# The last output chain moves into the first experts, the weight split into the attention, and two norms share one power

## The reference, cut to what matters

```python
h = W.T[x] + b + positional                       # embedding
h = h + linear_attention(layernorm(h))            # 8 heads of 16, normalised scores, causal
z = layernorm(layernorm(h), gain, bias)           # two norms in a row
q, k, v = z @ Wq, z @ Wk, z @ Wv                  # 2 heads of 64
q, k = l2norm(q) * 8 * qn_g, l2norm(k) * 8 * kn_g
y = causal_softmax(q @ k.T / 8) @ v @ Wo
gate = softmax(y @ gate_W + gate_b)               # over 8 experts
h = h + sum_e gate_e * (gelu(y @ W1_e + b1_e) @ W2_e + b2_e)   # 128 -> 512 -> 128
```

## Time and profile before

| | us |
|---|---|
| median of three runs (lowest, highest) | 964.89 (957.13, 965.5) |
| profiled execution, its time | 964.4 |
| its span | 962.3 |
| PE busy | 827.2 (86%) |
| DVE busy | 732.0 (76%) |
| ACT busy | 513.4 (53%) |
| POOL busy | 366.6 (38%) |
| mean granted clock of PE | 0.919 |

### The profile page before, as it was taken

One profiled execution on the slowest core, in us unless ns is written; L12 is line 12 of the kernel. 1 busy time (PEld: TensorE's weight loads), 2 busy tenths in 40 slices (PEclk: granted clock), 3 DMA queues, 4 the chain that ended last, 5 costly groups with the idle time before them and its releaser, 6 DMA issues.

```text
span 962.3 us, 21449 instructions
## 1 busy us (share of the span) xinstructions
PE 827.2 (86%) x7864; PEld 592.4 (62%) x7864; DVE 732.0 (76%) x1725; ACT 513.4 (53%) x1069; POOL 366.6 (38%) x478
## 2 busy tenths in 40 slices
PE   1677999999667565888898998699999999999997
PEld 1555777777433333556665666477777777777775
DVE  5736666666579896667667774399999999999997
ACT  1322444444056765667686898455555555555553
POOL 7565555555567774455565676100000000000000
PEclk9887999999656766899999999799999999999999
DMA  3110000000001110000000000000000000000000
GB/s 124 46 26 4 1 0 0 0 0 0 1 22 43 33 41 16 1 1 2 2 2 1 2 2 2 1 2 13 2 12 2 13 3 11 13 2 13 2 13 12
DMA packets 9474, 11.65 MB, mean 12 GB/s; under 512 B 1832, under 2 KB 6704, under 8 KB 9264
## 3 DMA queue, kind: packets, MB, share of 16 engines
q1 hardware_dynamic: 8368, 8.43, 2.9%
q0 software_dynamic: 1024, 2.10, 0.8%
HBM read 8.43 MB, written 2.10 MB: 11 GB/s over the span
## 4 chain that ended last, share of the span: by engine, by line
PE 60%; DVE 11%; POOL 11%; issue 9%; ACT 7%; DMA 0%; DVEq 0%; POOLq 0%; ACTq 0%
PE ps L897 59%; POOL plo L359 3%; DVE mx L794 2%; DVE y L684 2%; ACT phi L520 2%; POOL h_all L221 2%; ACT p L519 1%; POOL rr L306 1%; POOL rr L315 1%; DVE x L726 1%; DVE ss L732 1%; POOL ss L323 1%; ACT ql L506 1%; ACT arena L408 1%; PE ps L1167 0%
## 5 line engine op out<-in xcount | busy, mean ns | idle before, releaser
L897 PE MATMUL ps<-y,arena 128*128 128x512 f16 (+1 forms) x896 | 247.4, 424 | 19.3 <-DVE y L684 17.0
L548 ACT ACTIVATE cst<-ps,col 128x512 f32<-128x512 f32 x256 | 176.1, 688 | 163.6 <-PE ps L897 163.6
L897 PEld LDWEIGHTS ps<-arena,sq 128*128 128x128 f16 x3072 | 192.8, 98 | 60.5 <-DVE sq L883 0.7
L897 PE MATMUL ps<-arena,sq 128*128 128x128 f16 x3072 | 213.0, 219 | 0.5 <-DVE sq L883 0.5
L883 DVE TENSOR_TENSOR sq<-cst,sq 128x512 f16<-128x512 f32 x256 | 175.7, 686 | 4.4
L359 POOL TENSOR_TENSOR plo<-p,phi 128x512 f16<-128x512 f32 (+2 forms) x120 | 124.8, 1058 | 89.8 <-ACT phi L520 88.2
L878 DVE CAST sq<-cst 128x512 f16<-128x512 f32 x256 | 108.0, 422 | 12.2 <-ACT cst L548 3.1
L897 PEld LDWEIGHTS ps<-y,arena 128*128 128x128 f16 (+1 forms) x896 | 75.4, 112 | 58.5 <-issue 24.8
L794 DVE TENSOR_REDUCE mx<-ps 128x1 f32<-128x512 f32 (+3 forms) x160 | 91.3, 604 | 24.6 <-PE ps L897 23.8
L519 ACT ACTIVATE p<-ps 128x512 f32<-128x512 f32 (+3 forms) x160 | 88.2, 552 | 23.8 <-PE ps L897 22.6
L520 ACT ACTIVATE phi<-ps 128x512 f16<-128x512 f32 (+3 forms) x160 | 88.7, 554 | 0.0
(11 more groups left out here) (153 smaller groups left out, 1305.8 us busy)
## 6 DMA issues: line engine op xcount, KB each, us to landing
sq<-w_rows SPq DMA_DIRECT2D x16, 256.0 KB, 2.7
out<-h_all SPq DMA_DIRECT2D x32, 64.0 KB, 1.6
cst<-consts SPq DMA_DIRECT2D x1, 1294.0 KB
h_all<-emb_rows,idx POOLq DMA_INDIRECT x32
wqkv<-w_qkv SPq DMA_DIRECT2D x1, 192.0 KB
wsm<-w_sm SPq DMA_DIRECT2D x1, 192.0 KB
row<-rows SPq DMA_DIRECT2D x1, 140.0 KB
c<-consts SPq DMA_DIRECT2D x1, 96.0 KB
```

The costliest lines, as they stand in the source:

```text
L548: a.activation(hid[:, f], ps[:, HBANK[f], :], ACT.Gelu_apprx_tanh, bias=col[:, K_B1 + k:K_B1 + k + 1], scale=1.0 / WS).then_inc(S["hid_rea ...
L897: return t_.matmul(o, l, r, start=start, stop=stop, skip_group_check=True)
```

## The change

Three things. **One power for two norms**: the variance v of a row with mean removed becomes, after the first norm, v / (v + eps); so the two factors multiply to 1 / sqrt(v (1 + eps) + eps^2). DVE makes the bracket (`two_norms`), POOL one power. **The weight split** leaves the norm stage: ACT and POOL do the 16 pieces at the attention's steps 6, 14, ... 126 (`WSLOT`). The f32 copies lie in x2 and hxT, which are free by then; oT and y32 move to qkn. **The last block's output chain** (m = 7) is no longer behind the attention: its five parts stand behind given units of the experts on each engine (`PE_AT`, `ACT_AT`, `DVE_AT`, counted from unit 0), and the low part of y stands last on POOL. Bank 4 stays with it, so the up-projections use banks 0, 1, 5 and 6. The experts wait for a block's ylo and h2 only where they first use them. The other seven chains stay where they were (`out_part` is their code, unchanged, made a function).

```diff
--- before
+++ after
-        rr = [sb(f"rr{i}", [P, 4, B]) for i in range(2)]
-        x2 = [sb(f"x2{i}", [P, B, D]) for i in range(2)]
-        hxT = [sb(f"hxT{i}", [P, B, P]) for i in range(2)]
+        rr = [sb(f"rr{i}", [P, 2, B]) for i in range(2)]
+        x2_all = sb("x2", [P, 2, B, D])
+        hxT_all = sb("hxT", [P, 2, B, P])
...
-        scaled = [sqf[:, 1024:1536], sqf[:, 1536:2048]]
-        oT, y32 = scaled
+        scaled = [x2_all[:].rearrange("p i b d -> p (i b d)"), hxT_all[:].rearrange("p i b t -> p (i b t)")]
+        oT, y32 = (qkn[:, i].rearrange("p g z e -> p (g z e)") for i in range(2))
...
-        HBANK = [0, 1, 4, 5]
+        HBANK = [0, 1, 5, 6]
+        LAST = B * NQ - 1
```

On SP, the loads of the pieces:

```diff
-            with sp.Fori(2, NT - 1, 2) as n:
-                for u in range(2):
-                    sp.wait_ge(S["scaled_ready"], n + (u - 1))
-                    sp.dma_start(stage[u], w12_rows[:, ds(n * 512 + u * 512, 512)]).then_inc(S[STAGED[u]], 16)
+            for n in range(2, NPIECE):
+                sp.wait_ge(S["wlow_ready"], n - 1)
+                sp.dma_start(stage[n % 2], w12_rows[:, n * 512:(n + 1) * 512]).then_inc(S[STAGED[n % 2]], 16)
```

On POOL, both_norms and the split:

```diff
                 pool.wait_ge(S["stats2"], c + 1)
-                g.tensor_tensor(a, var, ln_eps, ALU.add).then_inc(S["rr_link"], 1)
-                g.tensor_tensor(b_, a, mhalf[:, 0:B], ALU.pow).then_inc(S["rr_link"], 1)
...
-                g.tensor_tensor(a, c_, mhalf[:, 0:B], ALU.pow).then_inc(S["rn_link"], 1)
...
-                g.tensor_tensor(rr[par][:, 3], a, b_, ALU.mult).then_inc(S["rr_ready"], 1)
+                g.tensor_tensor(rr[par][:, 1], rr[par][:, 0], mhalf[:, 0:B], ALU.pow).then_inc(S["rr_ready"], 1)
...
             def step_a2(c, par, left=3):
                 if left >= 1:
                     l2_factors(c + 1, 1 - par)
                 if left >= 3:
                     both_norms(c + 3, 1 - par)
-                weights_low(c, par)
...
+            def weights_low(n):
+                piece = w12[:, 4 * n:4 * n + 4]
+                pool.wait_ge(S["whigh_ready"], n + 1)
+                g.tensor_tensor(piece[:, :, 1, :], scaled[n % 2].rearrange("p (w d) -> p w d", d=D),
+                                piece[:, :, 0, :], ALU.subtract).then_inc(S["wlow_ready"], 1)
...
-            for k in range(NSTEP + LAG + 5 * YGAP + 3):
+            for k in range(NSTEP + LAG):
...
+                if k in WSLOT:
+                    weights_low(WSLOT.index(k))
-                for m in range(B * NQ):
+                for m in range(LAST):
                     if k == YAT[m] + 2 * YGAP:
...
+                        low_y(m)
+            low_y(LAST)
```

On ACT; step_a2 no longer calls weights_high, and the second hunk stands behind phi and max_row in each key step:

```diff
+            def weights_high(n):
+                act.wait_ge(S[STAGED[n % 2]], 16 * (n // 2 + 1))
+                a.activation(w12[:, 4 * n:4 * n + 4, 0, :], stage[n % 2].rearrange("p (w d) -> p w d", d=D),
+                             ACT.Copy, scale=WS)
+                a.activation(scaled[n % 2], stage[n % 2], ACT.Copy, scale=WS).then_inc(S["whigh_ready"], 1)
...
+                    if k in WSLOT:
+                        weights_high(WSLOT.index(k))
+                for m in range(LAST):
+                    out_part(m, (k - YAT[m]) / YGAP)
...
                     a.activation(hid[:, f], ps[:, HBANK[f], :], ACT.Gelu_apprx_tanh,
                                  bias=col[:, K_B1 + k:K_B1 + k + 1], scale=1.0 / WS).then_inc(S["hid_ready"], 1)
+                    if n * FT + f in ACT_AT:
+                        out_part(LAST, ACT_AT.index(n * FT + f) + 1)
```

On DVE:

```diff
-                last.then_inc(S["stats2"], 1)
+                last.then_inc(S["agg2"], 1)
+
+            def two_norms(c, par):
+                dve.wait_ge(S["agg2"], c + 1)
+                v.tensor_scalar(rr[par][:, 0], mv2[par][:, :, 1], 1.0 + LN_EPS, LN_EPS * LN_EPS, ALU.mult, ALU.add
+                                ).then_inc(S["stats2"], 1)
...
                 low_qk(c)
+                if left >= 3:
+                    two_norms(c + 3, 1 - par)
...
+                if r == 0 and n % E == 0:
+                    dve.wait_ge(S["h2_ready"], m + 1)
+                    dve.wait_ge(S["lg_link"], 5 * m + 5)
...
                     halves(n, f)
+                    if n * FT + f in DVE_AT:
+                        out_part(LAST, DVE_AT.index(n * FT + f) + 3)
```

On PE, and the places of the parts:

```diff
-            pe.wait_ge(S["split_done"], 2 + NPIECE)
-            pe.wait_ge(S["ylo_ready"], B * NQ)
-            pe.wait_ge(S["h2_ready"], B * NQ)
+            pe.wait_ge(S["wlow_ready"], NPIECE)
             pe.wait_ge(S["p_ready"], NSTEP)
+            pe.wait_ge(S["sm_used"], NMAX)
+            pe.wait_ge(S["o_used"], len(ITEMS) - 1)
...
                 pe.wait_ge(S["hid_ready"], n * FT + f + 1)
+                if n % E == 0 and f == 0:
+                    pe.wait_ge(S["ylo_ready"], n // E + 1)
...
                     down(n, f)
+                    if n * FT + f in PE_AT:
+                        out_part(LAST, PE_AT.index(n * FT + f) + 1)
...
+PE_AT, ACT_AT, DVE_AT = [1, 6, 11, 18, 23], [5, 10, 16, 22], [12, 16, 24]
+WSLOT = [8 * n + 6 for n in range(2 * E * FF // 512)]
```

More of the change, by code:

```diff
@@ L507, in max_row, with out_part @@
                        ).then_inc(S["mrow_sb"], 1)
+            def out_part(m, j):
+                if j == 1:
+                    act.wait_ge(S["oT_ps"], m + 1)
+                    a.copy(oT, ps[:, 4, :]).then_inc(S["oT_sb"], 1)
+                if j == 2:
+                    act.wait_ge(S["y_ps"], m + 1)
+                    if m:
+                        act.wait_ge(S["ylo_ready"], m)
+                    a.copy(y32, ps[:, 4, :])
+                    a.copy(yhi[:, m * CH:(m + 1) * CH], ps[:, 4, :]).then_inc(S["yhi_ready"], 1)
+                if j == 3:
+                    act.wait_ge(S["lg_ready"], m + 1)
+                    a.activation(gt[:, 1], gt[:, 0], ACT.Exp).then_inc(S["eg_ready"], 1)
+                if j == 4:
+                    act.wait_ge(S["gT_ps"], m + 1)
+                    a.copy(gT[:], ps[0:E, 4, :]).then_inc(S["gT_sb"], 1)
             max_row(0)
-            for k in range(NSTEP + LAG + 5 * YGAP + 3):
+            for k in range(NSTEP + LAG):
                 if k < NSTEP:
@@ L767, in _ @@
             stats2(2, 0)
+            two_norms(2, 0)
             normed2(1, 1)
@@ L860, in _ @@
-            dve.wait_ge(S["h2_ready"], B * NQ)
-            dve.wait_ge(S["lg_link"], 5 * B * NQ)
-            dve.wait_ge(S["split_done"], 2 + NPIECE)
+                for m in range(LAST):
+                    out_part(m, (k - YAT[m]) / YGAP)
+            dve.wait_ge(S["wlow_ready"], NPIECE)
             def add_rows(n, r):
@@ L1112, in scores, with out_part @@
                 last.then_inc(S["s_ps"], 1)
+            def out_part(m, j):
+                nonlocal bank4
+                if j == 1:
+                    pe.wait_ge(*bank4)
+                    pe.wait_ge(S["o_used"], 2 * m + 2)
+                    for r in range(4):
+                        last = t_.transpose(ps[:, 4, r * P:(r + 1) * P], och[:, r], ident)
+                    last.then_inc(S["oT_ps"], 1)
+                    bank4 = S["oT_sb"], m + 1
+                if j == 2:
+                    pe.wait_ge(*bank4)
+                    pe.wait_ge(S["oT_sb"], m + 1)
+                    mm(ps[:, 4, :], wo[:], oT).then_inc(S["y_ps"], 1)
+                    bank4 = S["yhi_ready"], m + 1
+                if j == 3:
+                    pe.wait_ge(*bank4)
+                    pe.wait_ge(S["yhi_ready"], m + 1)
+                    for r in range(4):
+                        last = mm(ps[:, 4, r * E:(r + 1) * E], y32[:, r * P:(r + 1) * P], wgate[:])
+                    last.then_inc(S["lg_ps"], 1)
+                    bank4 = S["lg_ready"], m + 1
+                if j == 4:
+                    pe.wait_ge(*bank4)
+                    pe.wait_ge(S["gate_ready"], m + 1)
+                    for r in range(4):
+                        last = t_.transpose(ps[0:E, 4, r * P:(r + 1) * P], gt[:, 3, r], ident)
+                    last.then_inc(S["gT_ps"], 1)
+                    bank4 = S["gT_sb"], m + 1
+                if j == 5:
+                    pe.wait_ge(*bank4)
+                    pe.wait_ge(S["gT_sb"], m + 1)
+                    for r in range(4):
+                        last = mm(ps[:, 4, r * D:(r + 1) * D], gT[:, r * P:(r + 1) * P], b2s[:])
+                    last.then_inc(S["b2_ps"], 1)
+                    bank4 = S["h2_ready"], m + 1
             def values(k):
@@ L1245 @@
 NSTEP = len(STEPS)
+NMAX = sum(len(p) for p in MPARTS)
+PE_AT, ACT_AT, DVE_AT = [1, 6, 11, 18, 23], [5, 10, 16, 22], [12, 16, 24]
+WSLOT = [8 * n + 6 for n in range(2 * E * FF // 512)]
 def on_pool(k):
```

161 lines of the change are left out of this document (45 added, 116 removed).

## The result

Changed kernel: 953.77 us (median of 15 runs, 948.56 to 957.98). Kernel before, on the same chips: 963.62 (957.13 to 966.63). The ratio is **0.9911 [0.9885, 0.9937]**, so 0.9% faster; predicted were 954.2 us. The interval excludes that nothing changed, but the gain is under the 1% from which the prediction counts a kernel as faster: it had given 0.54 to faster and 0.41 to this outcome. The profiled execution took 957.3 us, its span 955.1.

A forecast was written before the change was run, and what follows sets the result against it. It took DVE and POOL's loop to bound the norm steps, PE the experts with DVE close behind, and PE and ACT to be busiest in attention. 964.4 - 8.3 + 7.2 - 9.1 = 954.2 us, range 943 to 963.

The forecast's parts named there:

- (a): Norm stage: one power and no weight split there shorten DVE's step from 6.92 to 5.65 us at high clock; 8.3 us less.
- The front of the stage: Start of the norm stage: POOL's power no longer stands behind both_norms(0), so it comes 1.6 us earlier.
- (b): Attention: the weight split adds 1.04 us of ACT work at 16 key steps, partly covered by waits; 7.2 us more.
- R4: Rival, attention: ACT's 1.04 and POOL's 1.15 run in series, 2.2 us a slot, 35 in all, 982 us; chance 0.05.
- R2: Rival, attention: the split is not covered, all 16 slots pay 1.04, 16.6 us instead of 7.2, 963.6 us; chance 0.12.
- six covered slots: Attention slots 22, 30, 46, 62, 86, 110: ACT waits 0.69 us or more for a gate copy anyway, so cost nothing.
- The diagonal blocks: Attention after a change of item: narrow blocks make ACT wait 0.57 us, covering 1.7 us of slots 70, 94, 126.
- (c): Last output chain moved into the experts: hole 12.1 and start 1.9 gained, inserts 3.7 and stalls 1.2 lost; 9.1 us less.
- the table switches: Experts, unit 16: ACT loads the Exp table, then Gelu again, 1.28 us each, mostly hidden; 0.5 us lost.
- R3: Rival, experts: the table switches hold ACT, about 5 us more at unit 16, 957 to 960 us; chance 0.09.
- R5: Rival, experts: nothing changes, each insert waits as the old chain did with PE behind it, 963 us; chance 0.03.
- R1: Rival, norm stage: the shorter step keeps PE's clock high, 18 us less there, 944.5 us; chance 0.21.

The follow-up runs named there:

- with filling: Changed kernel plus eight matmuls per norm step whose result nobody reads: 939.22 us, 0.9770 of the kernel before.
- the other slots: Changed kernel with the 16 split pieces at other attention steps (12, 19, 24 and so on to 139): 948.47 us, 0.9881 of the kernel before.
- without the Exp: Changed kernel with the exp of the last block's gates replaced by a copy, so no table switch among the experts: 950.70 us, 0.9885 of the kernel before.
- the kernel with filling and the split back: Changed kernel plus eight unused matmuls per norm step, weight split put back into the norm stage: 932.48 us, 0.9706 of the kernel before.

## Why the prediction was right

**(a), predicted -8.3, seen -6.2 in the pair.** The mechanism held: DVE's wait and the long x went, the PE and ACT loop was late next at the low clock (6.76 to 6.98 us; 6.8 was said), and where the clock was high the steps came to 5.8 to 5.9 (5.65 was said, without any wait; with filling 5.68). Three things were off. The thirteen steps gave 3.7 us (90.0 to 86.3) instead of 6.7. The count of steps at the high clock was 3 in this execution, not 4.5; each lost step is 1.27 - 0.12 = 1.15 us, so 1.7 of the 3.0 missing, and the other 1.3 are steps 0.23 longer than said at the high clock and 0.07 at the low. The front of the stage, up to the second sum of squares, gave back part of it: 2.5 us less instead of 1.6. How many steps get the high clock is a matter of the execution: the same norm code ran at a clock of 0.56 here (6.64 us a step), 0.58 with the other slots (6.65) and 0.76 without the Exp (6.34, four steps near 6.0), and its stage took 124.6, 125.3 and 120.3 us, on average 7.3 less than before. And the step "weights_low leaves, so x falls from about 1.4 to 0.6" named the wrong cause. Before, both weights_low and x were let go by the same factor, the last of seven POOL operations, and so started together, at 313.53 and 313.70. With one power, ready early, they no longer do. The sum came out right because the fall was counted once; but it was booked as what moving the split brings, while the split brings nothing once there is one power. At the front of the stage POOL's power now starts 0.09 us behind DVE's variance (256.87 and 256.96) instead of 1.63, as predicted.

**(b), predicted +7.2.** In the pair +6.3. Over all profiles the attention takes 224.7 us on average with the split in it at the original slots (four kernels: 227.0, 223.5, 224.9, 223.5) and 217.8 without (six: 220.6, 220.7, 215.0, 219.5, 214.6, 216.6): +6.9. The timed ratios say the same: 0.9911 against 0.9842, and 0.9770 against 0.9706 with filling, which is 6.7 and 6.2 us (with filling the two intervals just overlap). R4 (35) and R2 as a whole (16.6) would have shown as an attention over 12 us longer; neither happened.

The total is right, the places and the way to it aren't. Cut the attention at the p of each slot's step, and most windows repeat from kernel to kernel within 0.02 us at a granted clock of 1.00. Others are longer, mostly by 1.3 to 1.6 us, at a clock of 0.86 to 0.88. Steps 86 to 94 without the split (one power only, then before), and steps 110 to 118 without it and with it (one power only, then split only):

```profile
502.12:513.82 11.70, 9.81 (x130) 6.75 (x129) 9.88 (x22) 7.77 (x19) 6.54 (x7) 1.00 0.01 1
509.26:522.59 13.33, 11.44 (x130) 7.43 (x129) 9.97 (x22) 7.87 (x18) 6.57 (x7) 0.87 0.00 1
534.29:544.92 10.63, 9.29 (x129) 6.56 (x125) 7.91 (x14) 8.07 (x19) 6.09 (x7) 1.00 0.01 2
540.15:552.42 12.27, 10.93 (x129) 7.29 (x125) 8.02 (x14) 9.48 (x22) 7.28 (x8) 0.86 0.08 23
```

The shortest of each window over the four kernels with the split at these places, less the shortest over the six without, gives what a slot costs (us; for slot 6 between executions whose window in front is equally long):

| slots | predicted, together | measured |
|---|---|---|
| 22, 30, 46, 62, 86 (in front of a gate copy) | 0 | 0, 0.2, 0.2, 0, 0 |
| 110 (the same) | 0 | 1.5 |
| 70, 94, 126 (partly covered) | 1.4 | 1.1, 1.1, 1.2 |
| 6, 14, 38 (partly covered) | 1.6 | 0.8, 0.3, 1.0 |
| 54, 78, 102, 118 (not covered) | 4.2 | 0.6, 0.7, 0.8, 0.8 |
| sum | 7.2 | 10.2 |

So five of the six covered slots are free, as said and against R2. The sixth isn't: in slot 110 the next p comes 0.7 us later, and then the clock is 0.86 in all four kernels with the split and 1.00 in all six without. The diagonal blocks cover nothing of 70, 94 and 126. And the 10.2 us became 6.9 on average because the windows at the lower clock lengthen an execution without the split by about 3.3 us more than one with it. The sum didn't have that term, and no run shows whether it is the split's doing or chance; that 7.2 fits so well is luck.

**(c), predicted -9.1, seen -9.7.** Hole closed (12.1), start 2.1 shorter (1.9 was said). From the first up-projection to the end it is 347.5 us instead of 345.0: 2.5 more, where 3.7 for PE's inserts and 1.2 for stalls less 1.9 make 3.0. The five units with an insert are 0.4, 0.9, 0.9, 0.5 and 1.2 us longer than the usual 1.32, 3.9 in all, which leaves 0.7 for stalls. The 0.5 for the table switches was 0. R3 falls: the load at 630.65 ends at 631.93 and the Exp starts at 631.95; the next load ends at 633.47 and the Gelu starts at 633.49. The 3.3 us without an activation behind the load of the earlier trace rows were a wait for PE. R5 falls with the chain-only kernel, 1.1% faster.

The Trainium skill (ScalarE: Activation LUTs, "What ACT_TABLE_LOAD costs") adds a drain of about 1.38 us to each load. The trace shows loads of 1.28 us with nothing behind them, and taking both out changed the stretch by 0.0 us. The measurement decides.

**R1**, that the clock keeps up, was right in what a kept clock would bring (5.65 said, 5.68 measured at 1.00) and wrong in that a shorter step keeps it: 0.56, 0.58 and 0.76 are not near 1.00. More work on PE did it.

**Sum.** The pair differs by 7.1 us (964.4 to 957.3), 2.4 less than its stages give, because the part in front, whose code is the same, took 2.4 us longer. The same code varies so: this part takes 251.8 to 255.9 us over all profiles, and the attention without the split 214.6 to 220.7, following the clock. The medians, 9.9 us apart, carry no such chance of one execution, and 10.2 less was forecast. That 954.2 was right to 0.05% is luck: the misses of (a), of (b)'s parts and of (c) cancel, and the kernel before itself had medians of 959.5 to 963.6 us in different groups of runs.

What stays open is why one execution keeps the high clock longer than another in the same norm or attention code; no run was made for it. A single pair of profiles can be off by 6 us in the attention and by 5 in the norm stage (120.3 to 125.3 us for the same code).

## What to carry to other kernels

Undo the parts of a bundle one by one: here a part that pays (one power), a part that costs as much (the split) and one that carries everything (the chain) looked like a single gain of 0.9%, and leaving out the bad one gives 1.6%. When two operations on two engines disturb each other, ask what makes them start together before moving one away. Unused matmuls that hold TensorE's clock pay 1.4% where PE's loop sets the pace and nothing where another engine does, so shorten the other loop first. Compare executions window by window between fixed instructions: here most windows repeat to 0.02 us, so one that is 1.3 to 1.6 us longer at a lower clock can be told from what an edit costs.

## What the runs showed of the hardware

**DVE and POOL.** Three DVE operations that start within a POOL operation on 512 elements end only when that has ended: the x pair 0.34 us behind POOL's end (315.02 and 314.68; 316.27 and 315.93 with filling), the small subtract 0.04 behind (533.24 and 533.20), and in the experts a cast, 1.29 instead of 0.42 us, 0.29 behind POOL's low part of y (624.74 and 624.45). Of the x pair it is the first operation that is held. It ends 0.09 us behind POOL's end in the step of the earlier trace rows, and 0.08 behind even where it starts 0.8 us into POOL's 1.16, in the kernel with filling and the split back: 315.27 and 315.19. It takes 0.42 instead of 0.34 there, because POOL is nearly done. A DVE operation that reads PSUM (unit_qk) also starts within that POOL operation and isn't held; it takes its usual 0.68 and ends at 314.93. The two, behind POOL's start at 314.03:

```profile
314.25 0.68 DVE L739 TENSOR_TENSOR qkn<-ps,ss 128x512 f32<-128x512 f32 x1
314.85 0.42 DVE L721 TENSOR_SCALAR x<-h_all,mv,rr 128x128 f32 x1
```

In every second step of the kernel before, the record of x starts 0.06 us ahead of POOL's, and still its first operation takes 1.29 us and ends 0.08 behind POOL's end:

```profile
320.44 1.29 DVE L726 TENSOR_SCALAR x<-h_all,mv,rr 128x128 f32 x1 [0.52 <-POOL rr L317]
320.50 1.15 POOL L334 TENSOR_TENSOR arena<-sq,arena 128x512 f32 x1
```

The Trainium skill (SBUF — State Buffer, "Who interferes with whom") says of a VectorE and a GpSimd operation that contend for the ports they share that whoever issues first holds them for its whole length and the other waits. The ends above agree, also those of the pair that took 0.67 (0.60 alone). By the records' starts x is first in every second step and yet waits; they don't show the order of issue.

**TensorE's clock.** It differs between executions of the same code: 0.56 to 0.76 over the thirteen steps with the changed kernel's norm code, between the levels of 1.2 and 2.4 GHz, and 0.87 or 1.00 in the same window of the attention, which is 1.3 to 1.6 us longer at 0.87 in most cases (11.70 and 13.33 us for steps 86 to 94). Eight unused matmuls a step raised it to 1.00 and made PE's busy time shorter, 52.5 instead of 61.9 us, with 288 matmul records instead of 184.
